# A two-layer graph network on one core: dense products of the first layer among the sums of the first stage, casts split by shape, weights in PSUM

## What is computed

```python
h = relu(layernorm(x))
msg = edge_weight * (h[dst] @ W_i + h[src] @ W_j + edge_attr @ W_e)
x1 = x + segment_sum(msg, dst) + h @ W_self
g1 = relu(layernorm(x1))
g2 = relu(segment_sum(g1[src], dst) / cnt @ W1_l.T + b1 + g1 @ W1_r.T)
y = segment_sum(g2[src], dst) / cnt @ W2_l.T + b2 + g2 @ W2_r.T
out = x1 + log_softmax(y)
```

## Time and profile before

| | |
|---|---|
| median of 3 runs | 1537.78 us (1536.27 to 1540.11) |
| profiled execution, its own time | 1539.19 us |
| span of its trace | 1536.8 us |
| PE busy | 1222.6 us (80%) |
| VectorE (DVE) busy | 1048.8 us (68%) |
| ScalarE (ACT) busy | 713.3 us (46%) |
| POOL busy | 1071.2 us (70%) |
| mean granted TensorE clock | 0.945 |
| first and last gather of the first stage | 52.0, 872.4 |
| first dense matmul | 884.6 |
| gathers of the layers | 901.6 to 1167.7, 1226.1 to 1496.7 |

### The profile page before, as it was taken

One profiled execution on the slowest core, in us unless ns is written; L12 is line 12 of the kernel. 1 busy time (PEld: TensorE's weight loads), 2 busy tenths in 40 slices (PEclk: granted clock), 3 DMA queues, 4 the chain that ended last, 5 costly groups with the idle time before them and its releaser, 6 DMA issues. The chain is left out here.

```text
span 1536.8 us, 27420 instructions
## 1 busy us (share of the span) xinstructions
PE 1222.6 (80%) x9615; PEld 990.7 (64%) x9615; DVE 1048.8 (68%) x2116; ACT 713.3 (46%) x1202; POOL 1071.2 (70%) x1044
## 2 busy tenths in 40 slices
PE   0157888888898898888875489888989888879887
PEld 0146677677787677767653277667777666667665
DVE  7776777987888788877786255545554655656565
ACT  3323544654565546554675143433333444434344
POOL 4777777777777777776777547777773077777770
PEclk9998999999999999999999699999999999999998
DMA  7478545665666556644577457656665755665663
GB/s 241 112 174 251 156 142 172 196 193 149 191 205 183 162 157 193 193 136 121 190 224 241 112 161 197 167 170 174 173 175 144 191 171 162 178 189 164 181 172 87
DMA packets 320509, 266.98 MB, mean 174 GB/s; under 512 B 32329, under 2 KB 297956, under 8 KB 320372
## 3 DMA queue, kind: packets, MB, share of 16 engines
q1 hardware_dynamic: 272708, 189.44, 42.1%
q0 software_dynamic: 33552, 69.34, 17.1%
q10 hardware_dynamic: 14112, 6.43, 1.5%
HBM read 212.08 MB, written 53.00 MB: 172 GB/s over the span
## 5 line engine op out<-in xcount | busy, mean ns | idle before, releaser
L852 POOL DMA_INDIRECT Dt<-h_d,idx x624 | 626.2, 1004 | 199.0 <-issue 189.6
L1458 POOL DMA_INDIRECT Dg<-g_d,idx x390 | 418.7, 1074 | 205.7 <-issue 148.2
L1419 PE MATMUL pc<-Kt,hi 128*128 128x512 f32 (+1 forms) x980 | 400.4, 412 | 14.5 <-issue 5.8
L1419 PE MATMUL pc<-Kt,lo 128*128 128x512 f32 (+1 forms) x980 | 382.4, 394 | 0.0
L1352 DVE CAST Kt<-Ut 128x2048 fp32r<-128x2048 uint8 (+3 forms) x168 | 234.4, 1402 | 53.1 <-PE pc L1419 44.1
L1247 ACT ACTIVATE Cb<-pc 128x784 uint8<-128x784 f32 x304 | 240.2, 823 | 50.9 <-PE pc L1235 48.6
L1419 PEld LDWEIGHTS pc<-Kt,hi 128*128 128x128 f32 x980 | 192.4, 196 | 57.9 <-issue 17.0
L1419 PEld LDWEIGHTS pc<-Kt,lo 128*128 128x128 f32 x980 | 191.9, 196 | 34.6
L1354 ACT ACTIVATE Kt<-Ut 128x1536 fp32r<-128x1536 uint8 (+3 forms) x112 | 181.6, 1623 | 64.4 <-PE pc L1419 55.8
L1209 DVE TENSOR_TENSOR Jt<-ps,keyT 128x1568 bf16<-128x1568 bf16 x204 | 196.5, 969 | 4.5 <-PE pc L1235 1.7
L1235 PE MATMUL pc<-Jt,Rt 128*128 128x196 bf16 x1216 | 148.4, 252 | 42.6 <-ACT Cb L1247 33.9
(11 more groups left out here) (155 smaller groups left out, 1545.9 us busy)
## 6 DMA issues: line engine op xcount, KB each, us to landing
Ut<-c_d SPq DMA_DIRECT2D x126, 448.0 KB
Dt<-in_ea SPq DMA_DIRECT2D x208, 192.0 KB
c_d<-Cb SPq DMA_DIRECT2D x38, 784.0 KB
Dq<-in_ea SPq DMA_DIRECT2D x77, 192.0 KB
Dt<-h_d,idx POOLq DMA_INDIRECT x624
g_d<-ht ACTq DMA_DIRECT2D x98, 64.0 KB
r_d<-rt SPq DMA_DIRECT2D x98, 64.0 KB
sp<-g_d SPq DMA_DIRECT2D x14, 448.0 KB, 4.8
```

What stands on the lines that cost most here:

```text
L852: e.indirect_dma_start(Dt[:, s, t, 0:128], None, h_d, bass.IndirectOffsetOnAxis(idx[:, c:c + 1], 0))\
L1419: last = e.matmul(pc[:, k % 2, 0:n], part[:, q, :], Kt[:, t % NK, j - q0, 0:n], start=(x == 0 and t % 2 == 0 and j == 0 and part is hi), s ...
L1458: e.indirect_dma_start(Dg[:, s, t, :], None, (g1_d, g2_d)[L], bass.IndirectOffsetOnAxis(idx[:, c:c + 1], 0)).then_inc(s_gg[s], 16)
```

## The change

1. **Counts and products in the first stage.** GE becomes 6, so the counts end two groups earlier. Among the last six groups, 27 of the dense units of the first layer are placed (NDEN), 3 more behind them. They belong to the first three chunks (AHEAD), row groups 0 to 4 (NX[0]). `units` is the new order: three chunks side by side, first NX of the 7 row groups, then the rest, then the other chunks. For the second layer NX is 4. Three accumulators in `pc` instead of two; the odd chunk goes to place 3; `apply_w` and `give_r` take other banks.
2. **Ring over the weighted matrix.** `Kt` has its place behind a pad of 83424 bytes, over Mt instead of over the first stage's `Dt`. A cast waits for the last `weigh`, the last level one of the own blocks and their sums, where it waited for the last level one.
3. **Casts.** ScalarE casts all four-row halves, VectorE all three-row halves. Before, of five units ScalarE had the second and fourth.
4. **Weights in PSUM.** Every fourth weighted unit copies three parts of 32 weights into `ps[3]`, and line 1217 (1206 before) reads them there.
5. **Second LayerNorm.** The shift by EPS goes into the square root's bias: one VectorE instruction a block less, with `ratio`, `newton`, `refined` in place of `newton1` to `3`.
6. **Checks.** The checks of the inputs and the flag stand behind the first LayerNorm instead of ahead of it.
7. **Pace.** START0, START1 are 0 and 4; `due` starts a layer's groups when its gathers are there.

```diff
@@ -42,11 +42,10 @@
-START0 = 15
+START0 = 0
 G0 = 1
-GE = 4
+GE = 6
 SUB = 8
-SPE = 4
@@ -56,8 +55,11 @@
-NSPL = 5
-START1 = 16
+NX = (5, 4)
+AHEAD = 3
+NDEN = 27
+KPAD = 83424
+START1 = 4
@@ -269,9 +272,10 @@
-        vs, mxs, sms, lns, Kt, Dg, Sg, Pg, gT, aT, ut, xe, x2, rl = scope(
+        pad, Kt = scope(("pad", [128, KPAD], U8), ("Kt", [128, NK, 4, 512], F32R))
+        vs, mxs, sms, lns, Dg, Sg, Pg, gT, aT, ut, xe, x2, rl = scope(
             ("vs", [128, NVS, VB, D], F32), ("mxs", [128, NB], F32), ("sms", [128, NB], F32), ("lns", [128, NB], F32),
-            ("Kt", [128, NK, 4, 512], F32R), ("Dg", [128, NDG, 12, D], F32), ("Sg", [128, NDG, 12, 32], F32),
+            ("Dg", [128, NDG, 12, D], F32), ("Sg", [128, NDG, 12, 32], F32),
@@ -1202,8 +1210,11 @@
                     own = R[:, 8 * (i % 2):8 * (i % 2) + 8, :]
+                    if m % 4 == 0:
+                        pair = wp[:, :, 8 * m:8 * m + 32, :].rearrange("p a w two -> p a (w two)").bitcast(F32)
+                        link(e, e.tensor_copy(ps[3][:, 256:352].rearrange("p (a w) -> p a w", w=32), pair))
                     for part, to in ((1, RW[:, m % 2, 0, :, :]), (2, RW[:, m % 2, 1, :, :]), (0, own)):
-                        e.tensor_tensor(pairs(to), pairs(own), each(wp[:, part, 8 * m:8 * m + 8, :], 64), ALU.mult)
+                        e.tensor_tensor(pairs(to), pairs(own), each(wpp[:, part, 8 * (m % 4):8 * (m % 4) + 8, :], 64), ALU.mult)
                 if i >= NJ:
@@ -1301,26 +1312,36 @@
-            chunks.insert(1, list(range(odd)))
+            chunks.insert(AHEAD, list(range(odd)))
         NCK = len(chunks)
         NI = NQG * NCK
+        units = []
+        for L in range(2):
+            for xs in (range(NX[L]), range(NX[L], NQG)):
+                units += [(L * NCK + c, x) for c in range(AHEAD) for x in xs]
+            units += [(L * NCK + c, x) for c in range(AHEAD, NCK) for x in range(NQG)]
+        unit_at = {u: i for i, u in enumerate(units)}
         HALF = ((0, 4), (4, 7))
         groups = list(range(first[BG], NG)) if BG < NB else []
         NGG = len(groups)
 
         def chunk_of(i):
-            return chunks[i // NQG % NCK]
-        unit_by = ["act" if t % 5 in (1, 3) else "dve" for t in range(4 * NI)]
+            return chunks[units[i][0] % NCK]
+        def q_group(i):
+            k, x = units[i]
+            return QO[k // NCK][x]
+        unit_by = [("act", "dve")[t % 2] for t in range(4 * NI)]
         unit_nth = [unit_by[:t + 1].count(unit_by[t]) for t in range(4 * NI)]
 
         def unit_done(e, t):
             e.wait_ge(s_kv if unit_by[t] == "dve" else s_ka, unit_nth[t])
 
         def load_counts(i):
-            qg = QO[i // NI][i % NQG]
+            qg = q_group(i)
@@ -1342,7 +1363,9 @@
                 if t < NK:
-                    e.wait_ge(s_p1, NGP)
+                    e.wait_ge(s_mm, 7 * (NB - BM))
+                    e.wait_ge(s_q1, NGQ)
+                    e.wait_ge(s_p2, max(seq[b] for b in range(BM, NB)) + 1)
                 e.wait_ge(s_u[i % NU], 16 * (i // NU + 1))
@@ -1411,12 +1434,12 @@
-                    if k >= 2:
-                        e.wait_ge(s_ge, k - 1)
+                    if k >= AHEAD:
+                        e.wait_ge(s_ge, k - AHEAD + 1)
                 for j in range(q0, q1):
                     q = QG * qg + j
                     for part in (hi, lo):
-                        last = e.matmul(pc[:, k % 2, 0:n], part[:, q, :], Kt[:, t % NK, j - q0, 0:n],
+                        last = e.matmul(pc[:, k % AHEAD, 0:n], part[:, q, :], Kt[:, t % NK, j - q0, 0:n],
@@ -1596,7 +1619,7 @@
-            p = pc[:, 2 + m % 2, 0:128]
+            p = ps[3][:, 0:128] if m % 2 else pc[:, AHEAD, 0:128]
@@ -1829,82 +1860,108 @@
                     more()
-                tick()
-                advance(99)
-                if g == NGP - 4 and u == 0:
+                for _ in range(1 if g < NGP - GE else 2 if g < NGP - 2 else 3):
+                    tick()
+                    advance(99)
+                if g == NGP - 1:
+                    break
+                if g == NGP - GE and u == 0:
+                    assert done[1] == len(parts)
+                    while extra:
+                        more()
                     for i in range(NU):
                         load_counts(i)
-                if g >= NGP - 4:
-                    j = (g - NGP + 4) * SUB + u
-                    if j % SPE == 0 and j // SPE < NSPL + 1:
-                        while j == 0 and extra:
-                            more()
-                        if j // SPE < NSPL:
-                            split_load(0, j // SPE)
-                        if j // SPE >= 1:
-                            split(0, j // SPE - 1)
+                if g >= NGP - GE:
+                    j = (g - NGP + GE) * SUB + u
+                    if j == 3:
+                        casts_to(NK - 1)
+                    if j % 3 == 0 and j // 3 < NX[0] + 2:
+                        if j // 3 < NX[0]:
+                            split_load(0, j // 3)
+                        if j // 3 >= 2:
+                            split(0, j // 3 - 2)
+                    while nden[0] < min((j - 9) * NDEN // ((GE - 1) * SUB - 9), NDEN):
+                        dense_unit()
         assert done == [len(octs), len(parts)] and not extra
-        def tail_step():
-            advance(1)
-            if ready or flight:
-                line.insert(0, tail_step)
-            else:
-                for x in range(min(NDG, NGG)):
-                    gather(0, x)
         for _ in range(12):
             tick()
+            advance(99)
         lag.clear()
         lag.update(LAG2)
-        casts_to(NK - 1)
-        line.append(tail_step)
-        for L in range(2):
-            clock = 0.0
-            start = (START0, START1)[L]
-            gnext = 0
-            for c in range(NCK):
-                k = L * NCK + c
-                for qg in range(NQG):
-                    i = k * NQG + qg
-                    if qg == 4:
-                        load_terms(L, chunks[c], 0)
-                    if c == 0:
...
-                    for t in (2 * i, 2 * i + 1):
-                        casts_to(t + NK)
-                        tick()
-                        dense(t)
+        pre = 2 * AHEAD * NX[0]
+        nsl = [NX[0], NX[0]]
+        while ready or flight or nden[0] < pre:
+            advance(1)
+            tick()
+            if nsl[0] < NQG and all((0, b) in turn_of for b in range(7 * QO[0][nsl[0]], 7 * QO[0][nsl[0]] + 7)):
+                split_load(0, nsl[0])
+                nsl[0] += 1
+            if nden[0] < pre:
+                dense_unit()
+        for x in range(min(NDG, NGG)):
+            gather(0, x)
+        for _ in range(8):
+            tick()
+        clock = 0.0
+        due = [START0, None]
+        gnext = [0, 0]
+        def given(L, y):
+            return all((L, b) in turn_of for b in range(7 * QO[L][y], 7 * QO[L][y] + 7)) and not follow
+        def rest_of_layer():
+            while gnext[0] < NGG:
+                take_group(0, gnext[0])
+                gnext[0] += 1
+                for _ in range(3):
+                    step()
+        for i in range(nden[0] // 2, 2 * NI):
+            k, x = units[i]
+            L, c = divmod(k, NCK)
+            if x == (NX[L] if c < AHEAD else 4):
+                load_terms(L, chunks[c], 0)
+            if c == 0:
+                if x == 0:
+                    nsl = [0, 0]
+                part = NX[L] if x < NX[L] else NQG
+                while nsl[0] < min(x + 3, part):
+                    if L == 1 and x >= NX[1]:
+                        rest_of_layer()
+                    while not given(L, nsl[0]):
                         step()
-                        clock += len(chunks[c]) * UC + UF
-                    while gnext < NGG and clock > start + PACE * (gnext + 1) + 3:
-                        take_group(L, gnext)
-                        gnext += 1
+                    split_load(L, nsl[0])
+                    nsl[0] += 1
+                while nsl[1] < min(x + 2, part):
+                    split(L, nsl[1])
+                    nsl[1] += 1
+            for t in (2 * i, 2 * i + 1):
+                casts_to(t + NK)
+                tick()
+                dense(t)
+                step()
+                clock += len(chunks[c]) * UC + UF
+            if due[1] is None and len(turn_of) == 2 * NB and not follow:
+                due[1] = clock + START1
+                for y in range(min(NDG, NGG)):
+                    gather(1, y)
+            for M in range(2):
+                while due[M] is not None and gnext[M] < NGG and clock > due[M] + PACE * (gnext[M] + 1) + 3:
+                    take_group(M, gnext[M])
+                    gnext[M] += 1
+            if x == NQG - 1:
                 while k >= 2 and k - 2 not in ll_of_chunk:
                     step()
                 take(k)
                 for b in chunks[c]:
```

(51 more changed lines are left out.)

58 lines of the change are left out of this document (27 added, 31 removed).

## The result

The changed kernel takes **1491.45 us** (median of 4 runs, 1490.82 to 1493.06), the kernel before 1538.59 beside it (4 runs, 1536.27 to 1540.11): ratio 0.9696, 95% interval 0.968 to 0.9713. Forecast were 1464 us, with a range of 1446 to 1504. Faster is right and the time lies in the range, but it is 27 us over the forecast, and two of the signs named for "wrong" came true: POOL goes on only after 925 (at 930), and TensorE's busy time changed by more than 15 us (by 20.9).

The account below looks back on a forecast made before the run. TensorE sets the first stage and, with POOL's stretched gathers, both layers. Last level one 893 + first layer 294 = 1187, + second layer 259 = 1446, + end 16 = span 1462; forecast 1464 us, range 1446 to 1504.

Parts of the forecast that it names:

- rival B: Layers: TensorE keeps its 64 us of waits, only their producer changes; 1504 us in full, 1484 at half; chance 0.18.
- Checks moved: Start of the first stage: moving the checks behind the first LayerNorm changes 0 us, bounds -1.5 to +4.
- Weights in PSUM: First stage: weighted products keep their duration, 0 us, bounds -10 and +20; POOL may be stretched less, also 0.
- rival C: First stage: weights from PSUM at the slow rate, +82 us on VectorE, some +20 in time, 1484 us; chance 0.05.
- Counts in 45 groups: First stage: denser counts delay group 38 by 18 us, POOL's last gather by 13, to 886; bounds +5 and +20.
- Products in the first stage: End of first stage: 42 us of products; last level one 893, POOL on at 906, +4, bounds -6 and +25.
- rival D: First stage runs long: count loads late, level ones behind them; POOL goes on at 926, 1484 us; chance 0.09.
- First layer: 294 us from last level one to last turned row, 893 to 1187; POOL starts the second layer at 1191.
- Second layer: TensorE needs 259 us instead of 286, keeping 12 us of waits, so the last group's product is at 1446.
- End: Behind the last group's product: 15.8 us instead of 28.9, as no dense products follow; span 1462.
- Casts: Layers: without long VectorE casts nearly all 52 us of stretched gathers go, booked once, in POOL's 1.25 us and TensorE's waits.
- Rival E: ScalarE's in-order queue holds casts behind copies, so TensorE misses operands: 106 us, 1570 us, slower; chance 0.06.

Follow-up runs that it names:

- e1: Kernel before with only the new division of casts (ScalarE all four-row halves, VectorE all three-row ones): 1504.54 us, ratio 0.977.
- e2: Changed kernel with the old division of casts (of five units ScalarE the second and fourth): 1532.07 us, ratio 0.996 against the kernel before.
- e3: Changed kernel with cast shapes swapped (VectorE all four-row halves, ScalarE all three-row ones): 1557.06 us, ratio 1.0134 against the kernel before.
- e4: Changed kernel with the checks and flag back ahead of the first LayerNorm: 1492.23 us, ratio 0.9701 against the kernel before.
- e9: Changed kernel with GE=4 and NDEN=12 instead of 6 and 27, so counts over 47 groups: 1485.74 us, ratio 0.9659 against the kernel before.
- e10: Changed kernel with NDEN=0 instead of 27: 1529.78 us, ratio 0.9947 against the kernel before.
- e12: Changed kernel with PACE=11.5 instead of 12, groups taken in earlier: 1517.2 us, ratio 0.9872 against the kernel before.
- e11: Changed kernel with the own blocks' weights read from SBUF again, without the copies: 1496.52 us, ratio 0.9738 against the kernel before.

## Why the prediction was right, and where not

**The range.** It held, but not for its reasons: its high end, 1504, stood there for rival B in full, and of the 29 us by which the span missed, 23 came from the first stage, which ran beyond the bound given to it (POOL's restart +28.7 us against the kernel before, bound +25). That the sum of the stages still fell inside is in part luck.

**What bounds it.** Right on casts and gathers: e1, e2 and e3 show the mechanism alone, in both kernels and in both directions. The Trainium skill's rule on the shared port pair (SBUF — State Buffer) holds here at 0.6 us a long cast. Why the short cast is spared: the trace gives the cast's input as 128 x 4 x 3 elements and the output as one run of 1536, the long one's as 128 x 4 x 4 and 2048. The Trainium skill (VectorE: DVE Perf Modes, on mode 2×_2P) asks for an outermost dimension that is even, or odd and equal in source and destination. The trace agrees: 1746 ns for three row blocks, 1234 for four. The casts of the small chunk of two blocks, in the kernel before, show the case of odd and equal:

```profile
L1352 DVE CAST Kt<-Ut 128x768 fp32r<-128x768 uint8 x10 | 7.0, 700 | 1.5 <-PE pc L1419 1.0 <-DMA Ut<-c_d 0.5
...
L1352 DVE CAST Kt<-Ut 128x1024 fp32r<-128x1024 uint8 x8 | 5.6, 696 | 1.1 <-DMA Ut<-c_d 0.8 <-issue 0.3
```

They too have three and four row blocks (128 x 2 x 3 and 128 x 2 x 4), but their destinations are 256 x 3 and 256 x 4, not one run. The one of 768 takes as long as the one of 1024, and less than half of the 1746 ns for 1536. So three row blocks alone don't make a cast slow; the slow one in these rows is the one with three row blocks on one side and a single run on the other. No kernel was run with another destination for it.

**Checks moved, 0:** right, by e4. **Weights in PSUM, 0:** right within what can be told; rival C falls with 679 ns instead of 1210. The Trainium skill's tier table (VectorE: DVE Perf Modes), which gives tensor_tensor with a PSUM operand the slowest mode, does not hold for this row.

**Counts in 45 groups: the step that failed.** It took 18 us by group 38, from the work alone, with bounds of +5 and +20 for the stage. Measured: 33, of which 15 are busy time, near the 18 sized, and 18 are waits, which the step held constant. Denser work in an in-order queue did not fill the gaps, it added some (e9). POOL's last 11 groups took 168.6 us instead of 165, so its last gather of the stage ended at 904.8 instead of 886, beyond my bound of 893.

**Products in the first stage:** level one of group 51 ended at 916.3 instead of 893, 12 us behind POOL's last gather, 23 late; the 14 us behind it were right (13). This is rival D's outcome (926, 1484 us; measured 930 and 1491), in the main with another cause: the counts themselves, 47 groups' worth in 45, which by 736 us had already cost 15 of the 23. D's own cause is there too, though, at 840 to 862: the first counts to be loaded wait for the last store (4.8 us), VectorE's and ScalarE's queues stand still for the load (6.7 and 7.5 us), and TensorE waits 6.1 us for the copy `Pt` behind ScalarE's casts. From 862 to the last level one TensorE is busy 52 of 54 us, so it had no idle time left to make that up. By e10, where POOL goes on 6.1 us earlier without the products, it can have cost some 6 us at most (an estimate); no run takes it apart.

**First layer:** 301 us from the last level one to the last turn, forecast 294. TensorE waits for no gather there, where 12 us were kept, but 10.1 for `ht` (ScalarE's rows of g2 to be turned), 7.4 for no named cause and 4.3 for `lo` (VectorE's low part of g1); rival B's shift of producer is real, at some 7 us of the 40 it would have cost. **Second layer:** 258.5 us, forecast 259. **End:** 14.9, forecast 16; by e12 the 56 products that no longer follow the last group are worth 19 us, not 13. The errors are 23.3 + 7.3 - 0.5 - 1.1 = 29, the whole distance from 1462 to 1491.0.

**Casts.** "Booked once" was right as a sum. What I missed is how much of the whole it was: with the new line the kernel before already has 34.5 of the 47 us. By the four medians, the other six parts together are worth 6.5 us beside the old line and 13 beside the new one; the 29 us lost in the first stage ate most of the 38 us that the products there gave (e10).

**TensorE's busy time.** It was taken as 1222.6 us and came to 1201.7. The matmuls are the same, the mean granted clock is 0.966 instead of 0.945; the 20.9 us are 1.7%, the clock 2.2%. The forecast had no term for it.

**Rival E** (ScalarE's queue) does not appear in the layers: TensorE waits 0.8 and 0.7 us for ScalarE's casts, though ScalarE casts 254 us.

## What to carry to other kernels

Before weighing engines against each other, look at what a fast instruction does to its neighbour: here a slower cast (1.75 instead of 1.23 us) on VectorE, with the long ones given to ScalarE, was worth 2.3% alone, and the faster one cost 0.6 us of POOL each. Read the chain by line for a helper engine's share first; 27% of gathers, nearly all of POOL's 418.7 us in the layers, said that most stretched microseconds count. When work is pressed into fewer steps of an in-order queue, size the waits with it, not the work alone.

## What was not expected of the hardware

Weights read from PSUM beside VectorE's products spare POOL as well, which the prediction had as a "may": the first stage's mean gather is 0.973 us with them and 1.001 without (e11), at the same 0.68 us a product. And one chip ran the kernel before in 2149 us instead of 1538, at a granted clock near 0.82; why was not found.
